# A graph network on one core: the build counts ten nodes a step, makes a pair's chunk one-hots and totals with one instruction each, and splits the input partly on GpSimd and ScalarE

## What is computed

```
h = relu(layernorm(x)); x = x + gin(h): twice mlp(h + segment_sum(h[src], dst))
h = relu(layernorm(x)); y = mlp3(h)[src]; z = segment_sum(y, dst)
out = x + mlp3(concat(h, z))
```

## Time and profile before

| | before |
|---|---|
| median of 3 runs | 1001.58 us (1000.74 to 1003.56) |
| the profiled execution | 999.83 us, its span 998.0 us |
| busy: TensorE, VectorE, ScalarE, GpSimd | 907.3, 743.3, 619.9, 312.9 us |
| build's last TensorE work ends | 410.0 us |
| granted TensorE clock, mean | 0.988 |

### The profile page before, as it was taken

One profiled execution on the slowest core, in us unless ns is written; L12 is line 12 of the kernel. 1 busy time (PEld: TensorE's weight loads), 2 busy tenths in 40 slices (PEclk: granted clock), 3 DMA queues, 4 the chain that ended last, 5 costly groups with the idle time before them and its releaser, 6 DMA issues.

```text
span 998.0 us, 25451 instructions
## 1 busy us (share of the span) xinstructions
PE 907.3 (91%) x11325; PEld 736.2 (74%) x11325; DVE 743.3 (74%) x807; ACT 619.9 (62%) x638; POOL 312.9 (31%) x204
## 2 busy tenths in 40 slices
PE   0159999999999999898999999999999979999995
PEld 0148888888888888545788888888888857777774
DVE  6999999999999999185565566565565566767672
ACT  1558898889888987244344444444444457777772
POOL 5657785858682300499920000000000000000000
PEclk9999999999999999899999999999999999999998
DMA  3024244424443344303444344433442447777761
GB/s 105 15 77 137 89 136 138 135 89 138 142 130 105 116 132 132 107 1 93 120 120 129 114 126 129 119 116 117 116 124 74 117 156 226 226 230 236 234 202 37
DMA packets 81377, 126.86 MB, mean 127 GB/s; under 512 B 9808, under 2 KB 58064, under 8 KB 81136
## 3 DMA queue, kind: packets, MB, share of 16 engines
q1 hardware_dynamic: 78128, 121.98, 39.9%
q0 software_dynamic: 3136, 3.22, 1.5%
HBM read 84.22 MB, written 40.94 MB: 125 GB/s over the span
## 4 chain that ended last, share of the span: by engine, by line
PE 50%; DVE 6%; ACT 1%; issue 1%; DVEq 0%
PE net_ps_hi L946 14%; PE net_ps_lo L946 14%; PE net_ps_hi L963 10%; PE net_ps_m L899 6%; PE net_ps_f L899 3%; DVE net_wide L603 2%; PE net_ps_hi L899 1%; ACT net_wide L829 1%; DVE hT L772 1%; DVE hT L774 1%; PE net_ps_m L998 1%; PE net_ps_t L907 1%; PE net_ps_t L993 1%; PE net_ps_lo L929 0%; DVE net_first L683 0%
## 5 line engine op out<-in xcount | busy, mean ns | idle before, releaser
L402 ACT ACTIVATE build_cnts<-build_ps_cnt 128x784 fp8e4<-128x784 f32 (+1 forms) x400 | 299.2, 820 | 52.7 <-PE build_ps_cnt L464 47.3
L603 DVE CAST net_wide<-net_raw 128x3584 fp32r<-128x3584 fp8e4 (+1 forms) x104 | 202.6, 1948 | 104.9 <-PE net_ps_lo L946 57.1
L829 ACT ACTIVATE net_wide<-net_raw 128x3584 fp32r<-128x3584 fp8e4 (+1 forms) x78 | 235.8, 3022 | 66.7 <-PE net_ps_hi L963 49.6
L946 PE MATMUL net_ps_hi<-net_wide,net_first 128*128 128x512 f32 (+1 forms) x637 | 249.3, 395 | 3.3 <-DVE net_first L684 3.3
L480 PE MATMUL build_ps_out<-build_parts,build_cnts 128*128 128x198 bf16 x2401 | 242.9, 250 | 0.0
L946 PE MATMUL net_ps_lo<-net_wide,net_first 128*128 128x512 f32 (+1 forms) x637 | 241.5, 383 | 0.0
L293 DVE TENSOR_TENSOR build_hot_lo<-build_grid_lo,build_keys_t 128x4096 bf16<-128x4096 bf16 x100 | 228.1, 2281 | 2.1 <-ACT build_keys_t L390 1.6
L480 PEld LDWEIGHTS build_ps_out<-build_parts,build_cnts 128*128 128x128 fp8e4 x2401 | 198.2, 98 | 8.1
L963 PE MATMUL net_ps_hi<-net_wide,net_second 128*128 128x512 f32 (+1 forms) x637 | 160.0, 403 | 2.5 <-ACT net_wide L829 1.6
L464 PE MATMUL build_ps_cnt<-build_hot_a,build_hot_lo 64*128 64x49 bf16 x6272 | 123.8, 184 | 29.6 <-DVE build_hot_a L293 24.3
L204 POOL DMA_INDIRECT build_edges<-in_edges,build_start_i x49 | 121.4, 2478 | 82.7 <-DVE build_hot_a L293 72.7
(11 more groups left out here) (145 smaller groups left out, 632.1 us busy)
## 6 DMA issues: line engine op xcount, KB each, us to landing
net_raw<-edge_counts SPq DMA_DIRECT2D x168, 448.0 KB, 3.5
edge_counts<-build_cnts SPq DMA_DIRECT2D x168, 224.0 KB
xres<-in_x SPq DMA_DIRECT2D x1, 1568.0 KB, 6.9
net_raw<-edge_counts SPq DMA_DIRECT2D x14, 112.0 KB, 2.0
out<-xres SPq DMA_DIRECT2D x12, 128.0 KB, 4.2
build_rows<-in_dst_rows,build_row_i POOLq DMA_INDIRECT x49, 4.2
build_edges<-in_edges,build_start_i POOLq DMA_INDIRECT x49, 5.1
edge_counts<-build_cnts SPq DMA_DIRECT2D x7, 112.0 KB
```

The costliest lines, as they stand in the source:

```text
L402: nc.scalar.activation(cnts[u % A_RING][:, 0:n, :, 8 * k:8 * k + 8], ps_cnt[b % CNT_RING][:, 0:n, 0:8 * NW].rearrange("p t (n a) -> p t a ...
L603: return issue(expanded[e % WIDE_RING][:, 0:n, :, :].rearrange("p w a d -> p (w a d)"), raw[e % RAW_RING][:, 0:n, :, :].rearrange("p w a d ...
L829: expand(act, lambda to, x: nc.scalar.activation(to, x, ACT.Identity), e).then_inc(grown["act"], 1)
L946: last = nc.tensor.matmul(ps[(b + 1) % 2][:, 0:n * P], first[:, c, lo:lo + H], expanded[e % WIDE_RING][:, 0:n, k, :], start=(c == 0), stop ...
```

## The change

Four things change, all in `build`:

- From pair 1 on a pair is counted in 13 steps, of ten columns each but for one of eight (step 2), and in six turns of 16 or 17 uses; pair 0 keeps 16 steps of eight. Keys of the next pair are turned at step 2 (pair 0: step 8) in place of 4 (12).
- The chunk one-hots of a pair are made by one instruction (`chunk_hots`) into one of two buffers; the lane one-hots stay in four groups. Both windows of a pair are totalled by one instruction (`total_pair`), for pair u - 3 after the first lane one-hots of pair u; `ps_out` has one bank for each pair.
- In the opening the squares are made window by window with their sum by ScalarE (49 instructions), the last subtraction is done by GpSimd ahead of the edges of group 2, and `find_keys(1)` comes before `find_starts(2)`.
- Later gathers are paced by `counted`, one every three steps.

```diff
-TURNS = [(0, 3)] + [(k, min(k + 2, STEPS)) for k in range(3, STEPS, 2)]
+SHORT = 2
+TURNS = [(0, 3), (3, 5), (5, 7), (7, 9), (9, 11), (11, 13)]
+PACE = 3
...
+def steps(u):
+    return 16 if u == 0 else 13
+def base(u):
+    return 16 + 13 * (u - 1) if u else 0
+def nodes_of(u, k):
+    if u == 0:
+        return range(8 * k, 8 * k + 8)
+    return range(10 * k - 2 * (k > SHORT), 10 * k + 10 - 2 * (k >= SHORT))
+def counted_with(s):
+    u, q = divmod(s, GROUPS)
+    return base(u) + 1 + max(k for k in range(steps(u)) if nodes_of(u, k).start < GROUP * (q + 1))
 def turn_step(u):
-    return 12 if u == 0 else 4
+    return 8 if u == 0 else SHORT
+def first_gather(g):
+    return base(FIRST_PAIR[g] - 4) + 2 if FIRST_PAIR[g] >= 4 else -13
...
-        hot_a = [sb(f"hot_a{i}", [P, GROUP, NA], BF16) for i in range(HOT_RING)]
+        hot_a = [sb(f"hot_a{i}", [P, P, NA], BF16) for i in range(2)]
-        ps_out = [ph.ps(f"ps_out{i}", [P, 512]) for i in range(2)]
+        ps_out = [ph.ps(f"ps_out{i}", [P, 2, 256]) for i in range(2)]
...
                 gather_rows(2, half, SPANS[2][1])
+                for q in range(4):
+                    pool.wait_ge(part1, q + 1)
+                    nc.gpsimd.tensor_tensor(parts64[:, shares[q], 2, 0:F], tmp[:, shares[q], :], parts64[:, shares[q], 1, 0:F],
+                                            ALU.subtract).then_inc(part2, 1)
                 gather_edges(2, *SPANS[2])
...
+                for t in range(base(NU)):
+                    for g in range(2, len(SPANS)):
+                        j, late = divmod(t - first_gather(g), PACE)
...
+                            pool.wait_ge(counted, t + 1)
+                            gather_edges(g, lo + j, lo + j + 1)
...
+                def chunk_hots(u):
+                    dve.wait_ge(keys_copied, u + 1)
+                    if u >= 2:
+                        dve.wait_ge(counted, base(u - 1))
+                    match(hot_a[u % 2][:, :, :], grid_a, 1, NA, u, 0, P)
+                def lane_hots(u, q):
+                    s = u * GROUPS + q
+                    if s >= HOT_RING:
+                        dve.wait_ge(counted, counted_with(s - HOT_RING))
+                    match(hot_lo[s % HOT_RING][:, :, :], grid_lo, 0, P, u, GROUP * q, GROUP).then_inc(hot_ready, 1)
+                def total_pair(u):
+                    n = both(u)
+                    dve.wait_ge(summed_out, 2 * u + n)
+                    v.tensor_reduce(sums[:, 2 * u:2 * u + n, :],
+                                    ps_out[u % 2][:, 0:n, 0:3 * FX].rearrange("p w (t f) -> p w f t", t=3), AX.X,
+                                    ALU.add).then_inc(totalled, 1)
...
                 find_keys(0)
-                norm_squares(0)
-                one_hots(0, 0)
+                chunk_hots(0)
+                lane_hots(0, 0)
                 find_starts(1)
-                for q in range(1, 4):
-                    norm_squares(q)
+                lane_hots(0, 1)
                 for q in range(4):
                     norm_invert(q)
                     norm_scale(q)
-                one_hots(0, 1)
+                lane_hots(0, 2)
                 for q in range(4):
                     norm_rest(q)
+                find_keys(1)
                 find_starts(2)
-                one_hots(0, 2)
-                for q in range(4):
-                    norm_last(q)
-                find_keys(1)
-                one_hots(0, 3)
+                lane_hots(0, 3)
                 for u in range(1, NU):
+                    chunk_hots(u)
                     for q in range(GROUPS):
-                        one_hots(u, q)
-                        if u >= 2 and q % 2 == 0:
-                            total_window(2 * u - 4 + q // 2)
+                        lane_hots(u, q)
+                        if q == 0 and u >= 3:
+                            total_pair(u - 3)
...
-                    nc.scalar.activation(tmp[:, w, :], h64[:, w, :], ACT.Square).then_inc(squared, 1)
+                    for t in range(w.start, w.stop):
+                        last = nc.scalar.activation(tmp[:, t, :], h64[:, t, :], ACT.Square, accum_out=stats[:, 2, t:t + 1])
+                    last.then_inc(squares_summed, 1)
+                    if q == 1:
+                        copy_first_keys()
```

108 lines of the change are left out of this document (45 added, 63 removed).

## The result

The kernel after the change takes 996.52 us (median of 16 runs, 994.16 to 999.75), the kernel before took 1000.95 us beside it (16 runs, 998.62 to 1003.56 but for one of 4588.71): a ratio of 0.9958, 95% interval 0.9947 to 0.9969. It is faster by 4.4 us; the forecast was 991 us, some 10 us less. The time lies inside the range of 985 to 997, near its slow end.

A forecast was written before the change was run, and what follows sets the result against it. VectorE paces pairs 2 to 15, TensorE the rest, within 2% of each other. Terms -1.4, -3.3, -3.8, -3.6, +0.9, +0.6 give -10.6 us: 999.83 becomes 989.2, with 1.75 to the median 991 us; range 985 to 997.

The forecast's parts named there:

- end of `find_keys(2)`: Opening: eighth edge gather issued at 71.1 us, landed at 75.6, so `find_keys(2)` ends at 78.0 for 79.44: -1.4 us.
- to the fourth group of pair 3: VectorE after `find_keys(2)`: 21.9 us for 25.1, pair 2's chunk instruction being made before the wait: -3.3 us.
- three periods of four pairs: VectorE's steady stage: merged instructions make 170.9 us into 3 x 55.7 = 167.1: -3.8 us.
- pair 16 to the end: TensorE's pace: nine pairs save 0.40 us each (-3.6), against +0.9 for one-hots at pair 16 and +0.6 for keys.
- the opening on GpSimd: GpSimd's late path: four subtractions, 7.7 us to 54.5, then eight edge gathers, one per one-hot instruction, before `find_keys(2)`.
- the first rival: GpSimd later still: subtractions wait for one-hots, `find_keys(2)` ends near 84, 6 us of gain go: 997 us; chance 0.14.
- The second: Opening: each GpSimd subtraction holds VectorE 1.9 us, `find_keys(2)` ends near 81.0, 3 later than forecast: 994 us; chance 0.10.
- The third: Opening: gathers are in time, so TensorE bounds; 7.5 us gained at pair 4 for 3.9: 987 us; chance 0.08.
- The fourth: Every pair: VectorE and TensorE wait in turns, 15.0 us a pair in place of 14.2: slower, 1013 us; chance 0.06.
- The fifth: VectorE's chunk one-hots: merging saves nothing (3.60 us), 0.2 us lost in each of 14 pairs: 993.5 us; chance 0.07.
- the wait at 71: Sign on VectorE: one wait of 4 to 6 us for gathered edges near 71 us; absent or over 10, forecast wrong.
- the forecast's two ends: ScalarE's small squares with sums: 0.3 us each just fits; at 0.61 us the keys come 7 us late.

The follow-up runs named there:

- second comparison: The changed kernel run once more, unaltered, against the kernel before: median of 11 runs 1001.09 us, ratio 0.9917.
- version with rows before edges: Changed kernel, subtractions back on VectorE, third group's second half of rows gathered ahead of second group's edges, `find_starts(2)` earlier: 989.61 us, ratio to kernel before 0.981.

## Why the prediction was wrong

Term by term, at the same marks (us, measured in the profiled executions):

| term of the sum | forecast | measured |
|---|---|---|
| end of `find_keys(2)` | -1.4 | 83.47 - 79.44 = +4.0 |
| to the fourth group of pair 3 | -3.3 | -3.2 |
| three periods of four pairs | -3.8 | (278.39 - 111.19) - 170.92 = -3.7 |
| pair 16 to the end (-3.6 + 0.9 + 0.6) | -2.1 | -2.3 |
| the build | -10.6 | -5.2 |

**The step that failed** is the opening on GpSimd, and in it the sentence against the first rival: "six of the 7.7 us lie beside `find_starts` and waits". I took work beside `find_starts` for hidden; it is where GpSimd's row and VectorE's two-input compare met. The row was shorter than forecast (6.33 us for 7.7), and one gather to a one-hot instruction and the landing (76.44 to 81.07, 4.6 us for 4.5) were right. What was missing is 4.9 us of hold. The subtractions ended as forecast (54.35 for 54.5), but the gathers behind them had to wait for `find_starts(2)` until 57.16; pair 1 started at 59.01 in place of 53.0, and the last gather was issued at 76.44 in place of 71.1. Putting the subtractions back took at least 4.5 us off the build and doubling them made the hold 6.2 us longer, so this cause is shown. The other 1.1 us of pair 1's delay are not traced; VectorE waited 2.17 us for the gathered rows ahead of the compare, 1.43 in the kernel before.

**The rivals.** The second named the mechanism, with 994 us; it priced the hold as 1.9 us a subtraction, on instructions that VectorE could still run in between, and found 3 us where 5.4 are. The Trainium skill ("SBUF — State Buffer", SBUF: two separate sides) has the ports held for the whole instruction by whichever starts first. The trace agrees that one side is blocked fully, but the compare waited for a row of four (of eight: 12.26 us) and not for one instruction; with gaps, and in the kernel before with the subtractions moved, it got in after one, as the page has it. The first rival's picture, each subtraction behind a one-hot instruction, came true only in the variants: where I delayed them past `find_starts(2)`, put waits between them, or moved them in the kernel before. The third is reached in part with the subtractions back on VectorE: the gathers are in time there, but VectorE and not TensorE still bounds. The fourth did not occur: VectorE idled for 0.4 us in all from 100 to 390 us. The fifth falls with the 0.20 us a pair.

**What was right.** 55.7 us for four pairs (55.74), the wait at the first group of pairs 4, 8, 12 and 16, turns of 2.2 us, first keys ready in time with 24 small squares at 0.24 us each (0.3 assumed). Two smaller things: the -3.3 of the table is 25.1 - 21.9 = 3.2 by its own working. And the 0.40 us a pair saved on TensorE came true (13.95 to 13.53) partly by luck: by the run with eight turns the turns gave 0.68, and the larger steps, taken at zero, cost 0.26. "It is wrong if the wait at 71 is absent" did not catch the miss: the wait was there, 3.55 us, but began at 77.5, some 7 us late.

Of the 5.5 us between 991 and the median, the opening accounts for 5.4. In the profiled executions 7.4 are missing (996.66 for 989.2), the further 2 in the rest of the span and around it, which varies by as much from one profiled execution to another. That the median of the first comparison fits so well is partly chance: the second comparison gave a ratio of 0.9917.

## What to carry to other kernels

Before work goes to GpSimd, look at what VectorE does in that very stretch, not at whether GpSimd has time: a gapless row of two-input GpSimd instructions can stop a two-input VectorE instruction until the row's end (it did in five traces and did not in one), and if the GpSimd queue behind the row needs that instruction's result, both lose. A long merged VectorE instruction is cheaper to run and lets fewer gathers in; its worth here was nothing that shows or 3.9 us, depending on whether gathers were late. Price a part of a change in the state that the other parts leave, and when two engines are within 2% of each other, relieve both.

## What the runs showed of the hardware

- Four GpSimd subtractions of two inputs (three of 768 elements a partition, mean 1583 ns, one of 832) back to back: the compare on VectorE 6.08 us in place of 1.23; eight of them: 12.26 us. Where VectorE's one-hots had begun first, or gaps lay between, a subtraction took up to 4.8 us and each that got in cost VectorE 1.4 us. In the kernel before with the subtractions moved, the row had no gap and the compare still waited for the first one alone (1.57 us).
- A gather on GpSimd's queue ended about 0.9 us after the next boundary between VectorE instructions, so its length (0.94 us beside an idle VectorE, up to 3.1) follows the lengths of VectorE's instructions.
- TensorE's granted clock fell to 0.50, the lower level (1.2 GHz), for 3 to 7 us in five traces, each time during or right after 40 count matmuls that came in pieces over 4.6 to 7.4 us (0.68 in the first trace), with late keys behind them; in the first trace of the changed kernel TensorE stood still for 3.05 us there, and the clock stayed at 1.00.
- ScalarE's sum beside an activation shows as an instruction of its own; the pair starts the next one after 0.24 us:

```profile
17.43 0.24 ACT L456 ACTIVATE build_cnts<-hT 128x64 f32<-128x64 f32 x1
17.58 0.19 ACT L456 ACTIVATION_READ_ACCUMULATOR build_cnts<-hT 128x1 f32 x1
17.67 0.24 ACT L456 ACTIVATE build_cnts<-hT 128x64 f32<-128x64 f32 x1
```

(ScalarE's timeline, version with rows before edges.) That answers the forecast's two ends, 0.3 and 0.61 us: it is below both.
